# Full fp32 products between the fp32r products of a first job: one row of eight against four pairs

## The chip, the cores and the metric

One core of one Trainium2 chip runs the kernel. The metric is device time in microseconds. The kernel before took 410.91 us, the median of three runs from 410.29 to 411.19.

## The reference

The input `x` has 1024 tokens of 512 features. Two layers follow each other, each a residual sum and a layer norm:

```python
approx_up = x @ up_w.T ; gate_pre = x @ gate_w.T          # 128 columns each, the "first job"
delta = gate_pre - local_point
approx_out = approx_up @ local_approx_output.T
for m in 1..6:                                            # terms: delta^m / m! times approx_up
    approx_out += (term_m * approx_up) @ fuse_weight[:, :, m-1].T
ffn = (silu(x @ ffn_gate_w.T) * (x @ ffn_up_w.T)) @ ffn_down_w.T      # 1248 rows
x = layernorm(x + approx_out + ffn)
dq_i = nf4_quant_dequant(w_i)                             # blocks of 64, codes of 16 levels
x = layernorm(x + (silu(x @ dq1.T) * (x @ dq2.T)) @ dq3.T)            # 1376 rows
```

All is fp32, and nearly every product is made of three fp32r products: high part by high part, high by low and low by high.

## The kernel before

Each engine has a program of its own, written out by hand, and semaphores tie them together.

**TensorE (PE)** does, in this order: five warm-up products (L1426); the first job, which is `up` and `gate` of the term part over four chunks `c` of 128 features (chunk 0 by L1435, L1438 and L1441, chunks 1 to 3 by `product`, L1292 to L1294); then twenty pairs, `pair(1, i)`, each a half of 512 tokens of the gate and the up product of one group of rows of layer 1's feed-forward; then the passes of the second products; then the same for layer 2. A product here is a weight load of 128 columns and a matmul over 512 tokens.

The first group of rows is special. It has 96 rows of gate and 96 of up. Gate's 96 and the last 32 of up are one fp32r job (`project_first`, job `("in", 0)`); the other 64 rows of up aren't split at all but multiplied in full fp32, by `project_up` (L1325 to L1332). It makes eight matmuls, two for each chunk: tokens 0 to 511 go to the lower 64 partitions of bank 5 and tokens 512 to 1023 to the upper 64, so the two use different halves of PE's columns. The trace shows each such matmul as two records. They stand after `project_first` of pair 0, and only after the last of them is `s_pair` raised for pair 0 (L1359 to L1363). The weights, 256 columns of `raw`, come with job `("in", 0)` in one transfer of 768 columns.

**ScalarE (ACT)** makes high parts (`w_hi`, `x_hi`, `l_hi`, all at L597 by `copy`), the silu of each pair (L680) and the lines of the NF4 steps (`side`, L635 and L597). **GpSimd (POOL)** makes low parts of weights (`w_lo`, L1236) and of `h` (L1247), multiplies layer 2's gate by up (L1254), and for NF4 the normalising (L1208) and the clamps (`level`, L1217). **VectorE (DVE)** multiplies layer 1's gate by up (L917 for the first two pairs, L920 after), makes the terms and adds up NF4 levels (L881, L885). **SyncE (SP)** issues nearly all transfers in one queue.

**What sets the order of the NF4 work.** The 136 NF4 steps (17 units of 8) have no place of their own. At each place where an engine would do a piece of the main work it first calls `beside()`, which does so many steps as the next number of a table, `SHARE`, says. There is one list for ACT, one for DVE and one for POOL.

PE may start pair `i` of layer 1, from the fourth pair on, when the product `h` of pair `i - 3` is made (L1346 to L1348), since it takes the banks of that pair. With `i = 3` it waits for two products of `h`.

## Time and profile before

| | us |
|---|---|
| median of three runs | 410.91 |
| lowest, highest | 410.29, 411.19 |
| the profiled execution | 410.27 |
| its span, first to last instruction | 408.2 |
| around the span | 2.1 |
| PE busy | 399.9 |
| POOL busy | 289.8 |
| DVE busy | 324.3 |
| ACT busy | 267.0 |

A row of the timeline gives the start, the length, the engine, the line, what was written and read, and in square brackets how long the engine sat idle before it and what released it. A matmul of 512 tokens is shown with 0.39 us although the next one starts 0.23 us later: they overlap in the pipe. So times on PE are read from starts to starts or from ends to ends. PEld is PE's weight load.

### The profile page before, as it was taken

Reading aid. Unit: us, or ns where it says so; the run is one execution under the profiler, and the core shown is the slowest. Engines: PE = TensorE matmul, PEld = TensorE weight load, DVE = VectorE, ACT = ScalarE, POOL = GpSimd, SP = SyncE. Lnnn points to the kernel's source line nnn. Section 1 sums busy time; section 2 is a strip of 40 time slices with the busy share of each in tenths; the row PEclk is TensorE's granted clock in tenths of the full one; section 3 lists DMA queues with packets and bytes.
Section 4 is the critical chain, followed back from the end, with each engine's and each line's share of the span. In section 5 each row is a group of like instructions: output and inputs, shape, how many; then the busy total and the mean of one; then the engine's idle time right before and its main releaser. Section 6 shows DMA issues by size and latency. Waiting matters only on the chain.

```text
span 408.2 us, 5342 instructions
## 1 busy us (share of the span) xinstructions
PE 399.9 (98%) x1762; PEld 325.8 (80%) x1762; DVE 324.3 (79%) x385; ACT 267.0 (65%) x372; POOL 289.8 (71%) x228
## 2 busy tenths in 40 slices
PE   8999999999999999999999999999999999999993
PEld 6767888888888888888888888888888877888872
DVE  4539889789889996999969799887789989925035
ACT  5574676686685847466955668887769777732613
POOL 0177998986978499737992465799999998954330
PEclk9999999999999999999999999999999999999998
DMA  8993111000104362003052000000000000000202
GB/s 276 406 408 126 53 22 51 28 26 0 53 20 116 92 213 71 26 0 104 1 167 112 0 2 0 0 2 0 2 2 0 2 0 0 2 1 0 104 0 103
DMA packets 10010, 26.42 MB, mean 65 GB/s; under 512 B 1248, under 2 KB 1632, under 8 KB 9728
## 3 DMA queue, kind: packets, MB, share of 16 engines
q1 hardware_dynamic: 9552, 25.30, 17.9%
q10 hardware_dynamic: 432, 0.79, 0.7%
q8 instruction: 14, 0.23, 0.2%
q14 instruction: 12, 0.10, 0.1%
HBM read 23.99 MB, written 2.10 MB: 64 GB/s over the span
## 4 chain that ended last, share of the span: by engine, by line
PE 95%; DVE 1%; POOL 1%; ACT 1%; issue 0%; POOLq 0%; DVEq 0%; ACTq 0%
PE PS L1292 31%; PE PS L1294 31%; PE PS L1293 31%; PE PS L1426 1%; PE PS L1330 1%; PE PS L1420 1%; POOL level L1217 1%; DVE h L917 0%; POOLq L262 0%; PE PS L1435 0%; DVE PS L885 0%; ACT side L635 0%; ACT side L597 0%; PE PS L1438 0%; PE PS L1441 0%
## 5 line engine op out<-in xcount | busy, mean ns | idle before, releaser
L1217 POOL TENSOR_SCALAR level<-side 128x1024 f32<-128x1024 int8 (+2 forms) x119 | 129.0, 1084 | 27.7 <-ACT side L597 15.4
L885 DVE TENSOR_TENSOR PS<-PS,level 128x1024 f32<-128x1024 f32 (+2 forms) x102 | 120.1, 1178 | 22.6 <-POOL level L1217 18.8
L1292 PE MATMUL PS<-x_hi,w_hi 128*128 128x512 f32 (+1 forms) x340 | 132.7, 390 | 0.3 <-DVE h L917 0.3
L1294 PE MATMUL PS<-x_hi,w_lo 128*128 128x512 f32 (+1 forms) x340 | 132.4, 389 | 0.0
L1293 PE MATMUL PS<-x_lo,w_hi 128*128 128x512 f32 (+1 forms) x340 | 132.3, 389 | 0.0
L597 ACT ACTIVATE side<-Q 128x1024 int8<-128x1024 f32 (+2 forms) x84 | 80.6, 998 | 22.1 <-DVE PS L881 18.0
L1247 POOL TENSOR_TENSOR l_lo<-h,l_hi 128x512 fp32r<-128x512 f32 (+1 forms) x42 | 57.3, 1374 | 26.5 <-ACT l_hi L597 25.8
L1292 PEld LDWEIGHTS PS<-x_hi,w_hi 128*128 128x128 f32 (+1 forms) x340 | 63.4, 186 | 15.1 <-issue 0.8
L1294 PEld LDWEIGHTS PS<-x_hi,w_lo 128*128 128x128 f32 (+1 forms) x340 | 63.4, 186 | 13.8
L1293 PEld LDWEIGHTS PS<-x_lo,w_hi 128*128 128x128 f32 (+1 forms) x340 | 63.4, 186 | 13.6
L1293 PE MATMUL PS<-x_lo,l_hi 128*128 128x512 f32 (+1 forms) x144 | 56.1, 389 | 0.0
L1292 PE MATMUL PS<-x_hi,l_hi 128*128 128x512 f32 (+1 forms) x144 | 56.1, 389 | 0.0
L1294 PE MATMUL PS<-x_hi,l_lo 128*128 128x512 f32 (+1 forms) x144 | 56.0, 389 | 0.0
L1236 POOL TENSOR_TENSOR w_lo<-raw,w_hi 128x1024 fp32r<-128x1024 f32 (+2 forms) x15 | 30.8, 2051 | 19.6 <-ACT w_hi L597 19.0
L680 ACT ACTIVATE h<-PS 128x512 f32<-128x512 f32 (+1 forms) x42 | 24.9, 592 | 29.1 <-PE PS L1294 25.9
L1254 POOL TENSOR_TENSOR h<-h,Q 128x512 f32<-128x512 f32 (+1 forms) x22 | 30.3, 1378 | 18.0 <-ACT Q L597 15.7
L597 ACT ACTIVATE l_hi<-h 128x512 fp32r<-128x512 f32 (+1 forms) x42 | 25.9, 626 | 24.9 <-PE PS L1294 24.8
L597 ACT ACTIVATE side<-raw 128x1024 int8<-128x1024 f32 x35 | 35.1, 1058 | 6.1 <-DVE PS L881 6.1
L1292 PEld LDWEIGHTS PS<-x_hi,l_hi 128*128 128x128 f32 (+1 forms) x144 | 27.0, 188 | 6.0 <-issue 0.2
L1292 PE MATMUL PS<-w_hi,l_hi 128*128 128x512 f32 (+1 forms) x80 | 31.5, 394 | 0.2 <-POOL l_lo L1247 0.2
L1294 PEld LDWEIGHTS PS<-x_hi,l_lo 128*128 128x128 f32 (+1 forms) x144 | 27.0, 188 | 5.7
L1293 PEld LDWEIGHTS PS<-x_lo,l_hi 128*128 128x128 f32 (+1 forms) x144 | 27.0, 188 | 5.5
(103 smaller groups left out, 515.2 us busy)
## 6 DMA issues: line engine op xcount, KB each, us to landing
Q<-w SPq DMA_DIRECT2D x10, 512.0 KB, 13.9
raw<-w_in SPq DMA_DIRECT2D x9, 512.0 KB, 9.9
raw<-w_out SPq DMA_DIRECT2D x13, 256.0 KB, 2.7
raw<-w SPq DMA_DIRECT2D x5, 512.0 KB, 3.9
R<-xN SPq DMA_DIRECT2D x2, 1024.0 KB, 6.4
raw<-w_fuse SPq DMA_DIRECT2D x7, 256.0 KB, 2.5
out<-R SPq DMA_DIRECT2D x7, 256.0 KB, 2.0
h<-xT SPq DMA_DIRECT2D x2, 512.0 KB, 7.0
```

The source lines that it names most:

```text
L597: return nc.scalar.activation(dst, src, ACT.Copy, **kw)
L680: nc.scalar.activation(dst, PS[0:dst.shape[0], bank, :], ACT.Silu).then_inc(s_silu, 1)
L885: v.tensor_tensor(total, total, level_of(s), ALU.add).then_inc(s_add, 1)
L1217: g.tensor_scalar(level_of(s), side_of(s), LIMITS[k][1], LIMITS[k][0], ALU.min, ALU.max).then_inc(s_level, 1)
L1236: g.tensor_tensor(lo, w_raw(j)[0:p, 0:n], hi.bitcast(F32), ALU.subtract).then_inc(s_wlo_in if JOBS[j][0] == "in" else s_wlo, 1)
L1247: g.tensor_tensor(lo, view, hi.bitcast(F32), ALU.subtract).then_inc(s_llo_h, 1)
L1254: g.tensor_tensor(dst, dst, up2[0:dst.shape[0], k % 2, :], ALU.mult).then_inc(s_h2, 1)
L1292: t_.matmul(dst, a_hi, b_hi, start=start, stop=False)
L1293: t_.matmul(dst, a_hi, b_lo, start=False, stop=False)
L1294: return t_.matmul(dst, a_lo, b_hi, start=False, stop=stop)
L1330: last = t_.matmul(PS[half * LEFT:(half + 1) * LEFT, UP_BANK, :], w[:, c, :], xT_raw[:, c, half * HALF:(half + 1) * HALF], start=c == 0, s ...
L1420: last = t_.transpose(PS[:, XT_BANK + t % 2, c * P:(c + 1) * P], R[:, t, c * P:(c + 1) * P], ident[:])
```

## The change

`project_up` is cut in four. Each call now makes the two matmuls of one chunk: chunk 0 after chunk 0 of the first job, chunk 1 after its chunk 1, chunk 2 after its chunk 2, and chunk 3 after the whole first job, before pair 0. `s_pair` is raised for pair 0 right after `project_first`. The 256 columns of weights have a transfer of their own, `up_raw`, which stands in SP's queue ahead of the second half of the first job's weights; the transfer of job `("in", 0)` has 512 columns left. A new semaphore, `s_up_made`, tells SP when the weights may be overwritten, in place of pair 0. All three lists of `SHARE` have new numbers with the same sum of 136.

```diff
 SHARE = {
     "scalar": [
-        0, 0, 0, 4, 0, 4, 1, 0, 3, 0, 2, 0, 0, 3, 0, 1, 2, 2, 1, 1, 3, 1, 0, 4, 4, 0, 1, 3, 0, 3, 3, 0, 3, 0,
+        0, 0, 0, 1, 2, 1, 2, 0, 1, 0, 5, 0, 0, 1, 0, 4, 0, 1, 3, 0, 3, 4, 0, 2, 4, 0, 2, 4, 0, 2, 2, 0, 4, 0,
...
                     if j - RAW_SLOTS == JOB["in", 0]:
 
-                        wait_pairs_done(sp, 1, 1)
+                        sp.wait_ge(s_up_made, 1)
                 p, n = job_shape(j)
                 if kind == "in":
                     first = 2 * DC * first_row1(f)
+                    if f == 0:
+
+                        n = DC * P
                     src = w_in[:, first:first + n]
...
                 if c == 2:
+                    sp.dma_start(up_raw, w_in[:, DC * P:2 * DC * REST]).then_inc(s_up_raw, 16)
                     sp.dma_start(w_raw(0)[:, 2 * PRE0:1024], w_pre[:, 2 * PRE0:1024]).then_inc(s_raw[0], 16)
...
-            def project_up():
-
-                w = w_raw(JOB["in", 0])[:, DC * P:2 * DC * REST].rearrange("p (c m) -> p c m", c=DC)
-                for c in range(DC):
-                    for half in range(2):
-                        last = t_.matmul(PS[half * LEFT:(half + 1) * LEFT, UP_BANK, :], w[:, c, :],
-                                         xT_raw[:, c, half * HALF:(half + 1) * HALF], start=c == 0, stop=c == DC - 1)
+            def project_up(c):
+
+                w = up_raw.rearrange("p (c m) -> p c m", c=DC)
+                for half in range(2):
+                    pe.wait_ge((s_x, s_xb)[half if c < 2 else 0][c], 16)
+                    last = t_.matmul(PS[half * LEFT:(half + 1) * LEFT, UP_BANK, :], w[:, c, :],
+                                     xT_raw[:, c, half * HALF:(half + 1) * HALF], start=c == 0, stop=c == DC - 1)
                 return last
...
                 if layer == 1 and i < 2:
-                    last = project_first(half, bank)
-                    if half == 0:
-                        last = project_up()
-                    last.then_inc(s_pair, 1)
+                    project_first(half, bank).then_inc(s_pair, 1)
                     return
...
             for c in range(1, DC):
+
+                if c == 1:
+                    pe.wait_ge(s_up_raw, 16)
+                project_up(c - 1)
                 if c == 1:
                     pe.wait_ge(s_pre_hi, 2)
                     pe.wait_ge(s_pre_lo, 2)
...
+            project_up(DC - 1).then_inc(s_up_made, 1)
             for i in range(2 * C1):
                 pair(1, i)
```

On PE before, the eight fp32 matmuls (`PS<-h,raw`, since the unsplit x lies in `h`) follow the last products of pair 0:

```order
L1292 MATMUL PS<-x_hi,w_hi 128x512
L1293 MATMUL PS<-x_lo,w_hi 128x512
L1294 MATMUL PS<-x_hi,w_lo 128x512
L1330 MATMUL PS<-h,raw 64x512 x8
L1292 MATMUL PS<-x_hi,w_hi 128x512
L1293 MATMUL PS<-x_lo,w_hi 128x512
```

On PE now, the first of the four pairs stands between chunk 0 (L1440 to L1446) and chunk 1 (L1300 to L1302) of the first job:

```order
L1440 MATMUL PS<-x_hi,w_hi 128x512 x2
L1443 MATMUL PS<-x_hi,w_lo 128x512 x2
L1446 MATMUL PS<-x_lo,w_hi 128x512 x2
L1338 MATMUL PS<-h,raw 64x512 x2
L1300 MATMUL PS<-x_hi,w_hi 128x512
L1301 MATMUL PS<-x_lo,w_hi 128x512
```

One row of eight has become four rows of two, with products of 128 columns before and behind each. The other three stand 12, 24 and 36 products further on.

On ACT before, around the first two silus (`h<-PS 96x512`), four NF4 lines stand between them:

```order
L597 ACTIVATE w_hi<-raw 128x1024
L680 ACT_TABLE_LOAD
L680 ACTIVATE h<-PS 96x512
L635 ACTIVATE side<-Q,line 128x1024
L597 ACTIVATE side<-Q 128x1024 x3
L680 ACTIVATE h<-PS 96x512
L597 ACTIVATE w_hi<-raw 128x1024
```

On ACT now, at the same place:

```order
L605 ACTIVATE w_hi<-raw 128x1024
L688 ACT_TABLE_LOAD
L688 ACTIVATE h<-PS 96x512
L643 ACTIVATE side<-Q,line 128x1024
L688 ACTIVATE h<-PS 96x512
L605 ACTIVATE side<-Q 128x1024 x2
L605 ACTIVATE w_hi<-raw 128x1024
```

Three of the four lines have left the place ahead of the second silu.

On DVE before, at the multiplications of gate by up of the first two pairs (L917, two instructions for each pair), two additions of NF4 levels stand ahead of pair 1's:

```order
L917 TENSOR_TENSOR h<-PS,h 32x512
L917 TENSOR_TENSOR h<-PS,h 64x512
L881 SCALAR_TENSOR_TENSOR PS<-side,level 128x1024
L885 TENSOR_TENSOR PS<-PS,level 128x1024
L917 TENSOR_TENSOR h<-PS,h 32x512
L917 TENSOR_TENSOR h<-PS,h 64x512
```

On DVE now, at the same place (L917 has become L925):

```order
L925 TENSOR_TENSOR h<-PS,h 32x512
L925 TENSOR_TENSOR h<-PS,h 64x512
L925 TENSOR_TENSOR h<-PS,h 32x512
L925 TENSOR_TENSOR h<-PS,h 64x512
L1101 SCALAR_TENSOR_TENSOR R<-R 128x2x512
```

Both additions have moved behind pair 1's multiplications.

## Rows read from the trace of the kernel before

**Rows 1.** The page: busy time by engine; the granted clock by slice.

```profile
PE 399.9 (98%) x1762; PEld 325.8 (80%) x1762; DVE 324.3 (79%) x385; ACT 267.0 (65%) x372; POOL 289.8 (71%) x228
...
PEclk9999999999999999999999999999999999999998
```

**Rows 2.** The waits of PE: line, waited for, us in total, times, longest.

```profile
PE PS L1426 <- POOL level L1257: 1.2, 1, 1.2
PE PS L1292 <- DVE h L917: 0.3, 1, 0.3
PE PS L1292 <- POOL l_lo L1247: 0.2, 1, 0.2
```

**Rows 3.** Timeline around the fp32 matmuls: start us, length us, engine, line.

```profile
19.18 0.39 PE L1293 MATMUL PS<-x_lo,w_hi 128*128 128x512 f32 x1
...
19.41 0.39 PE L1294 MATMUL PS<-x_hi,w_lo 128*128 128x512 f32 x1
19.73 0.20 PEld L1330 LDWEIGHTS PS<-h,raw 128*64 128x64 f32 x4 [0.35 <-issue]
19.73 3.65 PE L1330 MATMUL PS<-h,raw 128*64 128x512 f32 x16
20.21 0.14 PEld L1330 LDWEIGHTS PS<-h,raw 128*64 128x64 f32 x2 [0.29 <-issue]
...
22.36 0.14 PEld L1330 LDWEIGHTS PS<-h,raw 128*64 128x64 f32 x2 [0.28 <-issue]
...
23.31 0.50 PE L1292 MATMUL PS<-x_hi,w_hi 128*128 128x512 f32 x1
```

**Rows 4.** Timeline of PE around eight transposes of 128 columns.

```profile
192.59 0.39 PE L1294 MATMUL PS<-x_hi,l_lo 128*128 128x512 f32 x1
192.82 1.04 PE L1420 MATMUL PS<-ident,R 128*128 128x128 f32 x8
193.61 0.48 PE L1292 MATMUL PS<-w_hi,l_hi 128*128 128x512 f32 x1
```

**Rows 5.** Timeline of PE where the fourth pair of layer 1 begins.

```profile
31.38 0.39 PE L1294 MATMUL PS<-x_hi,w_lo 128*128 128x512 f32 x1
32.05 0.50 PE L1292 MATMUL PS<-x_hi,w_hi 128*128 128x512 f32 x1 [0.29 <-DVE h L917]
```

**Rows 6.** Timeline of ACT around the first two silus.

```profile
23.43 0.59 ACT L680 ACTIVATE h<-PS 96x512 f32<-96x512 f32 x1 [3.04 <-PE PS L1330]
23.92 1.14 ACT L635 ACTIVATE side<-Q,line 128x1024 int8<-128x1024 f32 x1
...
27.81 0.58 ACT L680 ACTIVATE h<-PS 96x512 f32<-96x512 f32 x1
```

**Rows 7.** Timeline of DVE: the multiplications of pair 1.

```profile
30.59 1.40 DVE L917 TENSOR_TENSOR h<-PS,h 32x512 f32<-32x512 f32 x2
```

**Rows 8.** Timeline of POOL: its first low part and first normalising.

```profile
19.17 2.37 POOL L1236 TENSOR_TENSOR w_lo<-raw,w_hi 128x1024 fp32r<-128x1024 f32 x1 [18.02 <-ACT w_hi L597]
21.49 1.90 POOL L1208 TENSOR_TENSOR Q<-Q,rcp 128x1024 f32<-128x1024 f32 x1
```

**Rows 9.** Timeline of ACT and PE while x and the first weights arrive.

```profile
7.74 0.63 ACT L597 ACTIVATE x_hi<-h 128x512 fp32r<-128x512 f32 x1 [0.37 <-DMA h<-xT]
...
8.76 0.39 PE L1292 MATMUL PS<-x_hi,w_hi 128*128 128x512 f32 x1
...
9.69 2.45 ACT L597 ACTIVATE x_hi<-h 128x512 fp32r<-128x512 f32 x4 [0.66 <-DMA h<-xT]
```

**Rows 10.** Timeline of PE at the last job of the last pass.

```profile
391.84 0.39 PE L1294 MATMUL PS<-x_hi,l_lo 128*128 128x512 f32 x1
...
392.43 0.47 PE L1292 MATMUL PS<-w_hi,l_hi 96*128 96x512 f32 x1 [0.20 <-POOL l_lo L1247]
```

**Rows 11.** Timeline of POOL: the low part of weights that the ninth pair takes.

```profile
56.74 2.39 POOL L1236 TENSOR_TENSOR w_lo<-raw,w_hi 128x1024 fp32r<-128x1024 f32 x1
```

**Rows 12.** Timeline of PE where the ninth pair begins.

```profile
59.39 0.39 PE L1292 MATMUL PS<-x_hi,w_hi 128*128 128x512 f32 x1
```

More of the change, by code:

```diff
@@ L326, in l_slot @@
             return l_hi[0:p, n % L_SLOTS, :], l_lo[0:p, n % L_SLOTS, :]
+        up_raw = w_raw(JOB["in", 0])[:, DC * P:2 * DC * REST]
         def job_shape(j):
@@ L363, in build @@
         s_lhi, s_llo_t, s_llo_h = sem("s_lhi"), sem("s_llo_t"), sem("s_llo_h")
+        s_up_raw, s_up_made = sem("s_up_raw"), sem("s_up_made")
         s_pre, s_up, s_delta = sem("s_pre"), sem("s_up"), sem("s_delta")
```

22 rows, old and new, of the table SHARE are left out of this document.

## The prediction, made before the changed kernel ran

> **What bounds the kernel now.** I read the page's first part first: PE is busy 399.9 us of a span of 408.2, the next engine, DVE, 324.3 [rows 1]. The waits of PE come second. Only three have a releaser: 1.2 us at the start, 0.3 for DVE in layer 1's pairs, 0.2 for POOL at the end [rows 2]. So the kernel is a string of PE work with almost no holes. A change can win only by taking work or a hole off PE, and loses what it adds there. The granted clock is at the top in nearly every slice [rows 1], and PE's work in the first microseconds stays as it is up to the first moved matmul, so I expect nothing from the clock.
>
> How large are the two holes inside? I take them from end to end, since ends follow each other by 0.23 us in the steady stream. At the fourth pair: (32.05 + 0.50) - (31.38 + 0.39) - 0.23 = **0.55 us** [rows 5]. At the last job: (392.43 + 0.47) - (391.84 + 0.39) - 0.23 = **0.44 us** [rows 10].
>
> **What the fp32 matmuls cost.** They take no time from anything else on PE, so their price is what they insert. From the last product before to the first behind, (23.31 + 0.50) - (19.41 + 0.39) - 0.23 = 3.78 us [rows 3]. Inside they are eight steps: the weight loads come by twos, at 20.21 and five steps on at 22.36, so a step is 0.43 us, and eight are 3.44 [rows 3]. Sixteen records in eight steps means that two always run together. What is left, 3.78 - 3.44 = **0.34 us**, is the price of going in and out once. Its signs are in the rows: the first loads start at 19.73, after 0.35 us without a load, and the product behind is shown with 0.50 us in place of 0.39 [rows 3].
>
> **Four visits in place of one.** The number of fp32 matmuls is the same, two for each chunk, thus two steps of 0.43. Each pair of them now stands between products of 128 columns, so the 0.34 is paid four times: a pair costs 0.86 + 0.34 = 1.20, four cost 4.80, against 3.78. That is **+1.02 us**, all on PE and so on the path.
>
> Is 0.34 the price of one visit however short? The lower bound is zero. Eight transposes between ordinary products insert (193.61 + 0.48) - (192.59 + 0.39) - 0.23 = 0.88 us, 0.11 each, which leaves next to nothing for going in and out [rows 4]; but they use all 128 columns, and the fp32 matmuls use 64. The upper bound is that two matmuls alone don't overlap as in a row of eight: four steps of 0.43 and 0.34 are 2.06 for a pair, 8.24 for four, which is +4.46. I take 0.34, since those rows are of the same instructions, and the first two records of the row already run together (four loads within the 0.20 us from 19.73 [rows 3]), without a predecessor of their own kind.
>
> The traced rows show a hole of 0.34 us around the 64-column matmuls and hardly one around the 128-column transposes. The Trainium skill, "TensorEngine Tiling (Array Packing)", section "Key Properties", says that changing the tiling mode, not just the tile, drains TensorE. It speaks against this change and gives no figure; if each change of mode drains, the sum is the +1.02 above, and if only long rows paid for it, 0.
>
> **The waits that the change adds on PE.** The first pair now waits for its weights. They are 128 KB in the same queue, ahead of the second half of the first job's weights. From 7.74, when the second half of x's chunk 1 is in, to 9.69, when chunk 2 is in, 256 KB of weights and 512 KB of x landed [rows 9]; that is 394 KB/us, so 128 KB take 0.33 us and are there at about 8.1. PE gets to them when chunk 0 of the job is done, at 8.76 [rows 9]. The cover is 0.7 us; without it PE would wait for what is missing. What stands behind in the queue (the weights of chunks 2 and 3, then x's chunks 2 and 3) lands 0.33 later, and PE asks for it 1.20 later, so it has gained cover. The total of bytes is the same, so the queue has caught up after job ("in", 0). The waits for x itself are old news: its high parts were made from it.
>
> **Who is later now.** The first job ends 3 x 1.20 = 3.6 us later. ACT's copy of up, its `w_hi` and POOL's `w_lo` for the second group hang on that: `w_lo` was there at 19.17 + 2.37 = 21.5 [rows 8] and will be at 25.1. PE wants it for pair 2, 12 products of 0.23 us behind the one at 23.31 [rows 3], at 26.1, now at 27.1. The cover shrinks from 4.6 to 2.0 us, and nothing is lost. SP's wait for `s_up_made` ends earlier than that for pair 0, but its queue is still busy with NF4 weights, so it gives nothing.
>
> **The hole of 0.55 at the fourth pair.** PE waits there for `h` of pair 1, which was made at 30.59 + 1.40 = 32.0 [rows 7]. On ACT four NF4 lines stand before pair 1's silu, which ended at 27.81 + 0.58 [rows 6], and on DVE two additions stand before its multiplications. The new table has one line and no addition there. Walked by rows: the products of pair 0 ended at 19.80 and now end 4.80 later, at 24.6, its silu 0.59 after that [rows 3, 6], at 25.2; POOL's `w_lo` ends at 25.1, its normalising of 1.90 [rows 8] at 27.0; ACT's one line of 1.14 [rows 6] to 28.2; the silu of pair 1, for which PE is done at 24.6 + 12 x 0.23 = 27.4, to 28.8; DVE's 1.40 to 30.2. PE gets there at 31.38 + 0.23 + 1.02 = 32.6 [rows 5]. So 2.4 us of cover where 0.55 were missing: **-0.55 us**.
>
> **The rest of the tables.** Before, some covers are thin: `w_lo` of the ninth pair was ready at 56.74 + 2.39 = 59.13, and PE took it at 59.39 [rows 11, 12], 0.26 us. Now two POOL steps fewer stand before it, and PE comes 0.5 us later. In the first pass of layer 1, DVE has two additions fewer before the low parts of the terms. In layer 2 the counts run within four steps of the old ones. I find no place where a step was put before something thin, but can't walk all 136, so I leave +0.0 in the sum and widen the range. The hole of 0.44 at the end stays: no NF4 step is near it, and ACT and POOL can start there only when PE frees a slot.
>
> **The sum.** +1.02 - 0.55 = **+0.47 us**. The profiled execution took 410.27, so it would take 410.7; it lies 0.64 below the median of 410.91, within their spread. On the median: **411.4 us**.
>
> **Rivals.**
> 1. *The new tables bring a wait of their own.* Another hole like the 0.55, or two, opens in the 290 us of pairs and passes, where DVE and POOL are busy 79% and 71% of the span [rows 1] and covers of 0.26 us exist. For it: the old tables left one such hole. Against: at the thin places I looked at, the counts went down. Price: +0.47 and 0.5 to 1.5 more, 411.9 to 412.9, slower. It decides from 0.35 us of new waits on.
> 2. *Two alone don't overlap fully.* In a row of eight, each half of PE's columns always has its next matmul at hand. The second matmul of a pair now carries a wait, and its second record may run alone. One step more for each pair is 4 x 0.43 = 1.72, thus 413.1; two steps more, +3.44, give 414.8. Against: the first two records of the row overlap too [rows 3].
> 3. *Going in and out is cheap for a short visit.* Then only the -0.55 stays: 410.4, still within 0.2%. For it only the transposes speak [rows 4].
> 4. *Faster.* Case 3 and the hole at the end goes too: -0.99, 409.9. It needs both.
> 5. *The change doesn't do what it says*: PE waits for `up_raw` and loses the overlap with the arriving data. With a cover of 0.7 us out of 0.33 us of transfer I give it no chance of its own; it would add some tenths.
>
> **How the numbers follow.** Forecast 50%, of which a fifth ends above 411.7 by small new waits; rival 1 20%; rival 2 10%; rival 3 10%; rival 4 and what I don't see on that side 10%. What a measurement of this kernel can tell from no change is about 0.2%, 0.82 us. Slower by more: 10 + 20 + 10 = 40%. Faster by more: 10%. Within: 50%. The range leaves out most of rival 2's far end and of rival 4: 410.3 to 413.1.
>
> **What would show it.** Right: in the timeline, four groups of four fp32 records, each inserting 1.2 us between the products around it, and the first at 8.8 to 8.9; the first job's end 3.6 us later; no wait of PE for DVE at the fourth pair; PE's busy time up by about 1 us, its idle time down by half a microsecond. Wrong: an insertion near 0.9 (rival 3) or 1.6 and more (rival 2); a row for PE in the waits that wasn't there, by POOL `w_lo`, DVE `l_lo` or DVE `w_lo` (rival 1); a wait of PE for the transfer of `raw` near 9 us (rival 5).

## The result, and the profile after

The changed kernel took **419.58 us**, median of five runs from 418.78 to 420.29. The kernel before took 410.86 beside it, five runs from 410.25 to 411.19. The ratio is 1.0215, with a 95% interval of 1.0195 to 1.0235. The forecast was 411.4, with a range up to 413.1: the kernel is 8.7 us slower where half a microsecond was foreseen. The profiled execution spans 417.1 us, against 408.2.

The page of the kernel after, to be held against [rows 1]: busy time by engine, and the granted clock by slice of 10.4 us.

```profile
PE 402.9 (97%) x1762; PEld 326.4 (78%) x1762; DVE 328.7 (79%) x385; ACT 267.0 (64%) x372; POOL 294.4 (71%) x228
...
PEclk9999999999999999999987999999999999999998
```

PE is busy 3.0 us longer, with as many instructions, and idle about 6 us longer. At slices 21 and 22 the clock isn't at its top, as it was before. The waits of PE, against [rows 2]: line, waited for, us in total, times, longest.

```profile
PE PS L1300 <- POOL l_lo L1255: 5.4, 3, 4.8
PE PS L1431 <- POOL level L1265: 1.2, 1, 1.2
PE PS L1440 <- ACT x_hi L605: 0.5, 1, 0.5
PE PS L1300 <- issue: 0.4, 1, 0.4
```

The wait for DVE's `h` is gone. POOL's `l_lo` is now waited for three times, once for 4.8 us; of the short two, one is the hole at the end that was there before. The 0.5 us for ACT's `x_hi` stand ahead of the first product and cost nothing: the last row of chunk 0 starts at 8.29, before at 8.30. The timeline of PE at the first and the fourth visit of the fp32 matmuls, against [rows 3]: start, length, engine, line.

```profile
8.83 1.08 PE L1338 MATMUL PS<-h,raw 128*64 128x512 f32 x4
9.84 0.50 PE L1300 MATMUL PS<-x_hi,w_hi 128*128 128x512 f32 x1
...
20.39 0.39 PE L1302 MATMUL PS<-x_hi,w_lo 128*128 128x512 f32 x1
20.71 1.08 PE L1338 MATMUL PS<-h,raw 128*64 128x512 f32 x4
21.72 0.50 PE L1300 MATMUL PS<-x_hi,w_hi 128*128 128x512 f32 x1
```

Each visit is four records in two steps. The last inserts (21.72 + 0.50) - (20.39 + 0.39) - 0.23 = 1.21 us, where 1.20 was foreseen. The three that start at 12.79, 16.75 and 20.71 are alike to the hundredth, and the first comes to 1.21 too. Four make 4.84 in place of 3.78: 1.06 us, where 1.02 was foreseen.

The timeline of PE where the time went:

```profile
214.03 0.39 PE L1302 MATMUL PS<-x_hi,l_lo 128*128 128x512 f32 x1
219.18 0.77 PE L1300 MATMUL PS<-x_hi,l_hi 128*128 128x512 f32 x1 [4.76 <-POOL l_lo L1255]
219.74 0.63 PE L1301 MATMUL PS<-x_lo,l_hi 128*128 128x512 f32 x1
...
222.73 0.63 PE L1302 MATMUL PS<-x_hi,l_lo 128*128 128x512 f32 x1
223.15 0.47 PE L1300 MATMUL PS<-x_hi,l_hi 128*128 128x512 f32 x1
```

The hole is (219.18 + 0.77) - (214.03 + 0.39) - 0.23 = **5.3 us** from end to end. Behind it eight products follow each other by 0.427 us in place of 0.228, and the ninth by 0.27: the clock stands at 1.2 GHz, half of its upper level, until 223.2. That is **1.6 us** more. The stretches of 1.7, 3.5 and 3.5 us there: busy time of PE, PEld, DVE, ACT and POOL with the number of instructions, then the granted clock, the DMA share and GB/s.

```profile
218.00:219.70 1.70, 0.52 (x1) 0.50 (x2) 1.59 (x2) 0.00 (x0) 1.62 (x2) 0.50 0.19 61
219.70:223.20 3.50, 3.50 (x10) 2.68 (x9) 3.50 (x5) 3.38 (x4) 3.34 (x3) 0.50 0.02 5
223.20:226.70 3.50, 3.50 (x17) 2.89 (x16) 2.84 (x7) 1.63 (x3) 2.15 (x3) 0.98 0.01 2
```

PE is fully busy in the second and third, but does 10 products in one and 17 in the other, at clocks of 0.50 and 0.98.

Two smaller holes are new:

```profile
81.47 0.39 PE L1302 MATMUL PS<-x_hi,w_lo 128*128 128x512 f32 x1
82.26 0.47 PE L1300 MATMUL PS<-x_hi,w_hi 128*128 128x512 f32 x1 [0.40 <-issue]
...
163.77 0.39 PE L1302 MATMUL PS<-w_hi,l_lo 128*128 128x512 f32 x1
164.65 0.47 PE L1300 MATMUL PS<-w_hi,l_hi 128*128 128x512 f32 x1 [0.49 <-POOL l_lo L1255]
```

They are 0.64 and 0.73 us. The sum: 1.06 for the visits, -0.55 for the hole at the fourth pair, 0.64 + 0.73, 5.3 and 1.6 make **8.8 us**, of 8.9 between the two spans.

**Back from the hole.** ACT's part of the chain:

```profile
216.15 1.02 ACT L605 ACTIVATE w_hi<-PS 128x1024 fp32r<-128x1024 f32 x1 [7.33 <-DVE PS L1036]
217.07 0.62 ACT L605 ACTIVATE l_hi<-h 128x512 fp32r<-128x512 f32 x1
```

PE waits for `l_lo`, that for `l_hi`. On ACT `l_hi` stands in the queue behind `w_hi`, which waited 7.33 us for a transpose on DVE. Its last microseconds on DVE:

```profile
202.23 2.07 DVE L852 TENSOR_REDUCE amax<-Q 128x16 f32<-128x1024 f32 x2
204.34 7.71 DVE L859 TENSOR_SCALAR rcp<-amax 128x32 f32<-128x32 f32 x1
212.08 0.35 DVE L861 RECIPROCAL rcp<-rcp 128x32 f32<-128x32 f32 x1
...
214.85 1.26 DVE L1036 STREAM_TRANSPOSE PS<-Q 128x1024 f32<-128x1024 f32 x1
```

Here is the cause's root: a `TENSOR_SCALAR` on 32 values per partition takes **7.71 us**. It is the floor of the block maxima (they are raised to the least normal number before the reciprocal). The same instruction in the kernel before:

```profile
201.55 0.64 DVE L851 TENSOR_SCALAR rcp<-amax 128x32 f32<-128x32 f32 x1
```

With POOL idle it takes 0.18 us, as at 73.73 in the kernel after. POOL in the kernel after at that time, and then in the kernel before:

```profile
199.98 1.90 POOL L1225 TENSOR_SCALAR level<-side 128x1024 f32<-128x1024 int8 x1
201.96 1.30 POOL L1255 TENSOR_TENSOR l_lo<-h,l_hi 96x512 fp32r<-96x512 f32 x1
203.22 1.30 POOL L1244 TENSOR_TENSOR w_lo<-raw,w_hi 128x512 fp32r<-128x512 f32 x1
204.48 1.29 POOL L1255 TENSOR_TENSOR l_lo<-h,l_hi 128x512 fp32r<-128x512 f32 x1
...
210.73 1.28 POOL L1244 TENSOR_TENSOR x_lo<-raw,x_hi 128x512 fp32r<-128x512 f32 x1
217.76 1.27 POOL L1255 TENSOR_TENSOR l_lo<-h,l_hi 128x512 fp32r<-128x512 f32 x1 [5.75 <-ACT l_hi L605]
```

```profile
202.09 1.29 POOL L1247 TENSOR_TENSOR l_lo<-h,l_hi 128x512 fp32r<-128x512 f32 x1
203.33 1.30 POOL L1236 TENSOR_TENSOR x_lo<-raw,x_hi 128x512 fp32r<-128x512 f32 x1
204.72 1.04 POOL L1217 TENSOR_SCALAR level<-side 128x1024 f32<-128x1024 int8 x1
```

In the kernel after the floor ends at 212.05, and POOL's six low parts from 204.48 on, which follow each other without a gap, end at 210.73 + 1.28 = 212.01. The new table has moved one clamp (`level<-side`) four places forward in POOL's row: it stood at 204.72, now it is the one at 199.98. The floor is a single-source instruction from SBUF to SBUF, and all of POOL's are in SBUF. The Trainium skill, "SBUF — State Buffer", section "Who interferes with whom", says that such an instruction of DVE in its two-port mode and GpSimd's share a port pair, that whoever issues first gets it for the whole instruction, and that the other fully blocks. That gives one instruction of waiting. The trace agrees with it at the other places (0.64 us above, and 1.28 at 152.38 in the kernel after, each to the end of the POOL instruction under way), but six more in a row are more than it says.

### The profile page after: what moved, and what is told of

It reads as the page before. It is cut to its first block, busy times and chain, and to the rows that moved or that the text cites. A ratio compares the mean times of both kernels' runs of the same rounds, so it can differ in the third digit from the quotient of the medians.

```text
span 417.1 us, 5344 instructions
## 1 busy us (share of the span) xinstructions
PE 402.9 (97%) x1762; PEld 326.4 (78%) x1762; DVE 328.7 (79%) x385; ACT 267.0 (64%) x372; POOL 294.4 (71%) x228
## 4 chain that ended last, share of the span: by engine, by line
PE 90%; issue 4%; POOL 3%; DMA 1%; DVE 1%; ACT 0%; POOLq 0%; DVEq 0%; ACTq 0%
PE PS L1300 30%; PE PS L1302 29%; PE PS L1301 29%; POOL l_lo L1255 2%; PE PS L1338 1%; DMA raw<-w_pre 1%; POOL x_lo L1244 1%; PE PS L1425 1%; POOL level L1225 1%; POOL w_lo L1244 0%; POOLq L262 0%; PE PS L1440 0%; PE PS L1443 0%; PE PS L1446 0%; ACT R L605 0%
## 5 line engine op out<-in xcount | busy, mean ns | idle before, releaser
L1225 POOL TENSOR_SCALAR level<-side 128x1024 f32<-128x1024 int8 (+2 forms) x119 | 131.5, 1105 | 36.8 <-DVE PS L893 14.7
L1300 PE MATMUL PS<-x_hi,w_hi 128*128 128x512 f32 (+1 forms) x340 | 133.1, 391 | 0.4 <-issue 0.4
L1302 PE MATMUL PS<-x_hi,w_lo 128*128 128x512 f32 (+1 forms) x340 | 132.4, 389 | 0.0
L1300 PEld LDWEIGHTS PS<-x_hi,w_hi 128*128 128x128 f32 (+1 forms) x340 | 63.4, 186 | 17.5 <-issue 3.2
L1302 PEld LDWEIGHTS PS<-x_hi,w_lo 128*128 128x128 f32 (+1 forms) x340 | 63.4, 186 | 13.9
L1300 PE MATMUL PS<-x_hi,l_hi 128*128 128x512 f32 (+1 forms) x144 | 57.0, 396 | 4.8 <-POOL l_lo L1255 4.8
L1302 PE MATMUL PS<-x_hi,l_lo 128*128 128x512 f32 (+1 forms) x144 | 56.8, 394 | 0.0
L1244 POOL TENSOR_TENSOR w_lo<-raw,w_hi 128x1024 fp32r<-128x1024 f32 (+2 forms) x15 | 31.8, 2117 | 22.4 <-ACT w_hi L605 21.7
L1300 PEld LDWEIGHTS PS<-x_hi,l_hi 128*128 128x128 f32 (+1 forms) x144 | 27.6, 191 | 11.0 <-issue 5.2
L1300 PE MATMUL PS<-w_hi,l_hi 128*128 128x512 f32 (+1 forms) x80 | 31.6, 396 | 0.7 <-POOL l_lo L1255 0.7
L1302 PEld LDWEIGHTS PS<-x_hi,l_lo 128*128 128x128 f32 (+1 forms) x144 | 27.5, 191 | 5.8
```

Source lines behind the costliest of these rows:

```text
L1225: g.tensor_scalar(level_of(s), side_of(s), LIMITS[k][1], LIMITS[k][0], ALU.min, ALU.max).then_inc(s_level, 1)
L1244: g.tensor_tensor(lo, w_raw(j)[0:p, 0:n], hi.bitcast(F32), ALU.subtract).then_inc(s_wlo_in if JOBS[j][0] == "in" else s_wlo, 1)
L1300: t_.matmul(dst, a_hi, b_hi, start=start, stop=False)
L1302: return t_.matmul(dst, a_lo, b_hi, start=False, stop=stop)
```

## The experiments

`SHARE` is the table that deals the NF4 steps out; an index is a place at which an engine takes so many steps. The ratios below are to runs of the kernel before on the same chip, whose medians lay between 410.44 and 410.72.

### Splitting the change in two

**The new order of PE with the old tables.**

```diff
-SHARE = { ... }    # the tables of after
+SHARE = { ... }    # the tables of before
```

> The changed kernel with the old tables: the four pairs of fp32 matmuls and the transfer of their own, but every NF4 step where it was. Theory S (a short VectorE instruction, the floor of the scales, waits while GpSimd runs a long row of two-input instructions, and the new tables made that row): the floor takes under 1.2 us again, no hole near 219 us, the four pairs insert 4.80 us in place of 3.78, and the wait at the fourth pair is back: 410.9 + 1.0 = 411.9 us. Rival O (the order of the fp32 matmuls itself brings the loss): 417 us or more.

Measured: 415.36, ratio 1.011 (1.0095 to 1.0125). The long floor isn't there (at most 1.13 us), but the time is 3.5 us above what was expected. PE and then ACT of this kernel:

```profile
35.21 0.50 PE L1300 MATMUL PS<-x_hi,w_hi 128*128 128x512 f32 x1 [2.40 <-DVE h L925]
...
36.52 0.63 PE L1302 MATMUL PS<-x_hi,w_lo 128*128 128x512 f32 x1
```

```profile
27.07 1.15 ACT L643 ACTIVATE side<-Q,line 128x1024 int8<-128x1024 f32 x1 [1.78 <-POOL Q L1216]
```

The hole at the fourth pair, 0.55 in [rows 5], is now 2.66 us. POOL's `w_lo` for the second group hangs on the end of the first job and comes 3.6 us later, and its normalising behind it; so ACT's first line begins at 27.07 and not at 23.92 [rows 6], 3.15 later, and with it the silu of pair 1 and DVE's multiplications. PE itself comes only 1.02 later: 0.55 + 3.15 - 1.02 = 2.68. The old table's four lines ahead of that silu can't stay with the new order; the forecast walked this chain for the new table alone. Some 1.3 us behind the hole the clock falls, and eight products from 36.52 on are at half speed, which adds 1.6. With 1.06 and 2.1 that is 4.8 us, as between the spans of 413.0 and 408.2.

**The new tables with the old order.**

```diff
-SHARE = { ... }    # the tables of before
+SHARE = { ... }    # the tables of after
```

> The kernel before with the new tables: the eight fp32 matmuls in one row behind pair 0. Theory S, if it hangs on the tables alone: the floor again takes 6 to 8 us, TensorE waits near 218 us, 418 to 419 us. Rival O: 410.4 us, the wait at the fourth pair gone and nothing else. Between the two, if the row of GpSimd is there but the floor comes at another moment of it: 410.4 plus what is left of the wait.

Measured: 418.58, ratio 1.0191 (1.0176 to 1.0206). The floor takes 7.72 us, the hole at 218.2 is 5.2 us, ten products behind it are slow. So the tables alone bring nearly all of the loss. The kernel after is 1.00 us above this one, and its span 0.9. That is near the 1.06 of the four visits, but the intervals leave about 1 us of play, and this kernel's hole at 81.3 is 1.02 us where the kernel after has 0.64. So the price of the visits rests on the rows above and not on this difference.

### Is it the floor, and is it the clamp?

**No floor.** This kernel leaves out the floor of the maxima of `w1` and `w2`; the reciprocal reads the maxima.

```diff
-                v.tensor_scalar(inverse, maxima, TINY, None, ALU.max).then_inc(s_floor, 1)
-                dve.wait_ge(s_floor, scaled(group[-1]))
-                v.reciprocal(inverse, inverse).then_inc(s_prep, 1)
+                v.reciprocal(inverse, maxima).then_inc(s_prep, 1)
```

> The changed kernel, its reciprocals for w1 and w2 read the maxima themselves; the floor of the scales (128x32, a guard against a block of zeros) is left out. Theory S: no hole near 219 us, no slow matmuls behind it; the 5.3 us and about 1.8 us of the lower clock go, 419.6 - 7.1 = 412.5 us. Rival L (the late low part of h is due to GpSimd's or ScalarE's own load, the long floor only stands beside it): at least 417 us.

Measured: 412.57, ratio 1.0046 (1.0029 to 1.0063). The hole at 219 and the slow products are gone, 7.0 us in all. The six floors left out take 0.18 us each where nothing holds them up. Holes of 0.36 and 0.34 us at 81.8 and 163.8 stay, and one of 0.9 at 181 is new.

**The clamp back in its old place.**

```diff
-SHARE["gpsimd"][34], SHARE["gpsimd"][38] = 1, 0
+SHARE["gpsimd"][34], SHARE["gpsimd"][38] = 0, 1
```

> The changed kernel with one number of GpSimd's table moved back: the clamp that stood between the low parts of the rows of out 0 and 1 in the kernel before stands there again, so the row of seven two-input instructions is cut in two. Theory S: the floor ends when the clamp comes, after about 4 us in place of 7.7, and TensorE's hole of 5.3 shrinks to under 2: 413 to 415 us. Rival R (what instruction GpSimd runs doesn't matter, only that it runs without a gap): the floor still takes 7 us or more, about 419.6 us.

Measured: 412.93, ratio 1.0055 (1.0038 to 1.0071). One step moved, in tables of 415 numbers, gives 6.7 of the 8.7 us back. The floor of this kernel:

```profile
204.00 0.63 DVE L859 TENSOR_SCALAR rcp<-amax 128x32 f32<-128x32 f32 x1
```

It got in as soon as the `l_lo` under way had ended, with the next low part ready behind it. The clamp, at 205.93, came later than that; it can't have been what opened the door.

**The floor three places later.** DVE's step that holds it goes behind the low parts of x and the transpose.

```diff
-SHARE["vector"][70], SHARE["vector"][73] = 3, 0
+SHARE["vector"][70], SHARE["vector"][73] = 2, 1
```

> The changed kernel, with one number of DVE's row moved: the NF4 step that holds the small floor of the scales (the 128x32 TENSOR_SCALAR that took 7.71 us at 204.34) comes three places later, behind the low parts of x and the transpose that wait in line after it; POOL's row is not touched, so its train of six low parts in a row stays. My theory (DVE is shut out of its small one-source instruction for as long as POOL's two-input low parts follow each other without a gap, and all behind it on DVE, then ACT, then POOL's l_lo, then PE, is late): the floor no longer meets the train, or meets it where nothing urgent stands behind; the hole of 5.3 us at 219 goes, and with it the half-clock products (1.75). 419.6 - 7.0 = 412.6, within 412.3 to 413.5. Rival A (the train itself is what makes PE wait, as POOL is behind by its own work, and the long floor is a symptom): the hole stays, 418 to 420. Rival B (the floor is long wherever it stands near POOL's work): a hole of several us at another place, 415 and more.

Measured: 415.36, ratio 1.0118 (1.0104 to 1.0132). Rival B's case: the floor met POOL's row at 209.14, took 4.09 us, to the end of what was left of the row, and the wait moved to DVE's `x_lo` and to the layer norm.

### What keeps the floor out?

Now the theory was that a row of POOL's without a gap shuts it out. It was put to the test by itself, with segments put behind the last store of the kernel before.

```diff
+            # POOL, ten times: a row of eight to twenty instructions
+            g.tensor_tensor(h[:, i * 512:i * 512 + 512], level[:, 0, 0:512], level[:, 1, 0:512], ALU.subtract)
+            # DVE, when the second has ended:
+            v.tensor_scalar(rcp[:, 0:1, :], amax[:, 0:1, :], TINY, None, ALU.max)
```

> The kernel before, and behind its last store ten short segments with nothing else running, which change no output. In each POOL runs a row of instructions without a gap (T: TENSOR_TENSOR 128x512 from two operands in SBUF, 1.25 us each; C: the clamp, a TENSOR_SCALAR 128x1024 from int8, 1.1 us each), and when POOL's second one is done, DVE gets one instruction to issue. Segments: 1 ten T, DVE the floor (TENSOR_SCALAR 128x32 SBUF to SBUF); 2 four T, a C, five T, the floor; 3 ten T, RECIPROCAL 128x32; 4 ten T, TENSOR_TENSOR 128x32; 5 ten T, the floor's TENSOR_SCALAR with its source in PSUM; 6 eight C, the floor; 7 ten T, TENSOR_SCALAR 128x512; 8 ten T, TENSOR_TENSOR 128x512 from two operands in SBUF; 9 ten T, two floors in a row; 10 twenty T, the floor. My theory (DVE's instruction is shut out until POOL's row has a gap or an instruction of another kind): in 1 the floor ends with the tenth T, about 10 us; in 2 with the C, 2.5 to 3.5 us; in 3 and 5 0.2 to 0.4 us; in 6 under 1.3 us; in 7 as 1; in 10 about 22 us. For 4 and 8 the trace shows low parts on DVE stretched from 0.69 to 1.6 us, so I expect up to a few us. In 9 the second floor is quick, since the row is over by then. Rival (POOL and DVE take turns, one instruction each, and the 7.71 us came from something else that was under way, such as a transfer or ACT): the floor takes at most 1.4 us in every segment.

The theory fell. DVE's instructions of segments 1, 3, 5 and 8: start, length.

```profile
411.09 1.15 DVE L1215 TENSOR_SCALAR rcp<-amax 128x16 f32<-128x16 f32 x1 [2.67 <-POOL h L1325]
...
435.97 0.25 DVE L1217 RECIPROCAL rcp<-amax 128x16 f32<-128x16 f32 x1 [11.32 <-POOL h L1325]
...
460.79 0.17 DVE L1221 TENSOR_SCALAR rcp<-PS 128x16 f32<-128x16 f32 x1 [11.30 <-POOL h L1325]
...
494.87 1.63 DVE L1225 TENSOR_TENSOR Q<-Q 128x512 f32<-128x512 f32 x1 [11.22 <-POOL h L1325]
```

The floor waits for the one instruction under way, and gets in ahead of POOL's next. So does a `TENSOR_TENSOR` of two SBUF operands. A `RECIPROCAL` and a floor that reads PSUM didn't wait. The section of the Trainium skill named above has two kinds of instruction contend, `tensor_scalar` in its two-port mode and `tensor_tensor` with both inputs in SBUF. The probe agrees with it on both, and on the length: one instruction. The section doesn't name `RECIPROCAL`.

**Does the moment of arrival decide?** Three runs asked that: a probe that swept it, and two kernels in which a dummy `RECIPROCAL` delays the floor.

```diff
+                v.reciprocal(Q[:, 5 + k // 5, at:at + n], Q[:, 4, at:at + n])    # n from 10 to 160
                 ins = v.tensor_scalar(rcp[:, 0:2, :], amax[:, 0:2, :], TINY, None, ALU.max)
```

> The kernel before, and behind its last store 27 short segments with nothing else running, which change no output. In each POOL runs eight TENSOR_TENSORs 128x512 in a row (SBUF, 1.22 us from start to start); when the second is done, DVE runs a RECIPROCAL over n elements as a delay and then the floor (TENSOR_SCALAR 128x32, SBUF to SBUF), so that the floor comes at a chosen age of POOL's instruction: n from 10 to 160, ages 0.3 to 1.2 us. Segments 17 and 18 take a TENSOR_TENSOR in place of the floor, 19 reads from PSUM, 20 to 27 repeat n = 100 to 142 with POOL writing fp32r behind a wait, as in the kernel. The last probe took from my theory that a row of POOL's instructions shuts the floor out as such: arriving 0.15 us after POOL's start it ended with that one instruction. What the traces of the kernels show is an age: arriving 0.04 to 0.06, 0.70 to 0.74 or 1.3 of 2.4 us after POOL's start the floor ended with that instruction; at 1.00 (e5, 4.09 us) and 1.12 (after and the tables alone, 7.71) it ended with the whole row; at 1.175 it slipped in and took 0.18. New theory (the age decides: one that comes when POOL's instruction is nearly done, with the next already asking, loses every turn): floors at ages 1.0 to 1.13 take 5 to 6 us, to the end of the eight, the others 1.22 minus the age. Rival (the age is not it; something of the kernel's own, such as waits, fp32r or work of ACT and DMA beside it, is needed): all floors take at most 1.3 us, or only those of 20 to 27 are long.

All 24 floors from SBUF got in after at most one instruction, at ages from 0.02 to 1.21 us (the age is the time since POOL's instruction under way had started). The row below has shortest, median and longest in ns, then the start of the first and the last.

```profile
L1211 DVE TENSOR_SCALAR rcp<-amax x24: 117/320/1020, 411.3 to 672.3; 128x32 f32<-128x32 f32 x24
```

```diff
                 if group == SCALE_GROUPS[-1]:
+                    v.reciprocal(delay[:, 1, 0:22], delay[:, 0, 0:22])
```

> The changed kernel with 0.2 us of idle work added: a RECIPROCAL over 22 elements, of which nothing is used, ahead of the two reductions that precede the long floor; tables and order stay. In the kernel after, the floor came 1.12 us after the start of POOL's TENSOR_TENSOR of 1.29 us, 0.14 before the next one's start, and took 7.71 us; floors that came at ages of 0.04 to 0.06 and 0.70 to 0.74 ended with that one instruction. Theory (the age decides in the kernel, though the probe did not show it): 0.2 later it comes 0.06 us after the start of the next one and takes 1.3 us; the hole at 219 goes, 412.3 to 413.5. Rival (this place, with its six low parts in a row, shuts it out at any age): 418.5 to 420.

Measured: 420.08, ratio 1.0238 (1.022 to 1.0255). The floor came some 0.15 us later against its neighbours: not 1.12 us into POOL's instruction but 0.01 into the next. It took 7.56 us.

The same, with 54 elements, in the kernel before:

> The kernel before with 0.4 us of idle work added, a RECIPROCAL over 54 elements ahead of the same two reductions. Its floor came at 201.55, 0.72 us after the start of POOL's TENSOR_TENSOR, and took 0.64 us. Theory (the age decides): now at an age of about 1.12, it loses every turn until POOL's clamp, which starts at 204.72 in this order: it takes 2.5 to 3.0 us. PE has cover for this there: 410.4 to 411.5. Rival (the age does not matter): 0.2 us or one instruction of POOL, at most 1.4 us, 410.4 to 410.8. The time hardly tells them apart, the length of the floor in the trace does.

Measured: 410.4, ratio 1.0006 (0.9992 to 1.0019). The floor came at an age of 1.08 us, near the 1.12 of the kernel after, and took 0.31. So age isn't it.

**Is it what the probe left out?** The third probe put a reduction and a semaphore ahead of the floor, gave POOL's instructions fp32r outputs and waits of their own, and let ACT copy beside them.

```diff
+                v.tensor_reduce(amax[:, 0, 0:12], Q[:, 3, 0:768].rearrange("p (b e) -> p b e", e=BLOCK), AX_X, ALU.max,
+                                apply_absolute_value=True).then_inc(s_red, 1)
+                dve.wait_ge(s_red, k + 1)
                 ins = v.tensor_scalar(rcp[:, 0:2, :], amax[:, 0:2, :], TINY, None, ALU.max)
```

> The kernel before, and behind its last store 26 segments that change no output, made more like the place in the kernel: the floor has a TENSOR_REDUCE 128x768 ahead of it and waits for it by a semaphore. POOL runs eight TENSOR_TENSORs 128x512; the first one's end starts DVE, which runs a RECIPROCAL over n elements (10 to 176), the reduction and the floor, so that ages from 0.1 to 1.2 us are met. 1 to 10: POOL as in the last probe. 11 to 18: POOL writes fp32r from two tensors, each instruction behind a wait of its own. 19 to 26: the same, with eight copies of 128x512 on ACT beside it. Theory (an age of 1.0 to 1.13, in conditions like the kernel's, loses every turn): at the ages near 1.1 the floor takes 4 to 6 us in all three kinds, or in the later ones alone, which then names the condition. Rival (a condition that this probe also lacks, such as PE or DMA): none over 1.3 us.

None of 26 took over 1.29 us. The rival holds.

**Is it the shared port?**

```diff
-v.tensor_scalar(inverse, maxima, TINY, None, ALU.max)
+v.tensor_scalar(*(t.rearrange("p u b -> p b u") for t in (inverse, maxima)), TINY, None, ALU.max)
```

> The changed kernel, complete, with the floor of the scales reading and writing its 128x32 values in another order: inner step 16 elements in place of 1. Nothing else moves. Theory (the floor waits because, contiguous and from SBUF to SBUF, it runs in a mode that needs the port that DVE shares with POOL): with a step it doesn't need the port, takes some 0.2 us at 204.3 although POOL's six low parts still stand beside it, and the hole of 5.3 us and the half-clock products go: 419.6 - 7.1 = 412.5, within 412.2 to 413.2. Rival (it is not the port but something else at this place that keeps the instruction for 7.7 us): the floor stays at 7 us and the time at 419 to 420.

Measured: 419.57, ratio 1.0216 (1.0199 to 1.0233); the floor took 7.72 us. That doesn't speak against the port, since the next probe showed that a step doesn't free the instruction from it: alone beside POOL's row, the stepped floor took 0.6 and 1.0 us like the other.

**Is it what came before?** In after, e2, e5, e8 and e10 the clamp ahead of the row had itself been held up by DVE (1.90 us for 1.04, at 199.98); where the floor got in, a low part had been.

```diff
+                # POOL: two low parts, then the clamp that DVE holds up, then eight low parts
+                v.scalar_tensor_tensor(sum_, side[:, 1, :], LIMITS[0][1], level[:, 2, :], ALU.min, ALU.add)
```

> The kernel before, and behind its last store 20 segments that change no output. In all four kernels in which the floor was shut out (after, the tables alone, e5, e8) POOL had, in the same run of work, a clamp (single source) that itself had been held up by a DVE instruction with two operands in SBUF (1.90 us in place of 1.04, at 200.0); where the floor passed (before, e1, e4, e9) a two-operand instruction of POOL had been held up (2.27 us). Each segment repeats that: POOL runs two TENSOR_TENSORs, then X, then eight more; DVE issues an instruction with two SBUF operands during the second (the addition that the kernel has, or a TENSOR_TENSOR), so that X is held up; then a RECIPROCAL, the reduction, a delay and the floor. 1 to 6: X is the clamp, 7 to 12: X is a TENSOR_TENSOR; in each three with the one holder and three with the other, delays 20, 90, 150. 13: a holder with one operand. 14 to 18: X the clamp, and in place of the floor a RECIPROCAL, a TENSOR_TENSOR, the floor from PSUM, the floor with a step (twice). 19, 20: the floor with other delays. Theory (a clamp held up leaves DVE out of turn from then on): floors of 1 to 6 and 19, 20 take 4 to 8 us, those of 7 to 12 at most 1.3. Rival (history does not matter either): none over 1.3 us. In both cases 14, 16, 17 and 18 take 0.1 to 0.4 us.

The clamps were held up as in the kernel, 1.90 us; no floor took over 1.18.

**One clamp in the kernels.** First the old kernel with the clamp where the new table has it, then the new kernel with the clamp one place further back:

```diff
-SHARE["gpsimd"][34], SHARE["gpsimd"][38] = 0, 1
+SHARE["gpsimd"][34], SHARE["gpsimd"][38] = 1, 0
```

> The kernel before with one number of POOL's row changed: the clamp that stands four places behind, between two l_lo, comes ahead of them, as in the new table; DVE's and ACT's rows and the fp32 matmuls stay. In this order POOL has six low parts in a row beside the floor. Theory (this one move is enough): the floor takes 5 to 8 us, PE waits some 4 to 5.5 us near 210 and runs some products at half clock, 410.6 + 5 to 7 = 415.5 to 418. Rival (it takes the other moved steps as well): floor at most 1.3 us, 410.4 to 411.5.

Measured: 411.36, ratio 1.0016 (1.0005 to 1.0027). The rival holds: the floor took 0.65 us, with a gapless row beside it that was longer than in the kernel after. The time is 0.6 us up, with a new hole of 0.8 us at 233.6, where PE waits for an `x_lo` of DVE's.

```diff
-SHARE["gpsimd"][34], SHARE["gpsimd"][35] = 1, 0
+SHARE["gpsimd"][34], SHARE["gpsimd"][35] = 0, 1
```

> The changed kernel with the same clamp one place further back (behind the next l_lo, ahead of w_lo), so that it is no longer the instruction that DVE's addition holds up; behind it there are still six low parts in a row beside the floor. Theory A (that the clamp was held up at 200.0 is the condition for the long floor): the floor takes at most 1.3 us, 412.5 to 413.5. Theory B (the row of six without a clamp is the condition, in the kernel if not in the probes): the floor takes 6 to 8 us and the time is 418.5 to 420.

Measured: 412.26, ratio 1.0048 (1.0032 to 1.0065), 7.3 us less for one clamp moved by one place. DVE and POOL of this kernel:

```profile
203.87 0.33 DVE L859 TENSOR_SCALAR rcp<-amax 128x32 f32<-128x32 f32 x1
```

```profile
201.74 1.05 POOL L1225 TENSOR_SCALAR level<-side 128x1024 f32<-128x1024 int8 x1
202.87 1.30 POOL L1244 TENSOR_TENSOR w_lo<-raw,w_hi 128x512 fp32r<-128x512 f32 x1
204.12 1.30 POOL L1255 TENSOR_TENSOR l_lo<-h,l_hi 128x512 fp32r<-128x512 f32 x1
...
211.63 1.29 POOL L1255 TENSOR_TENSOR l_lo<-h,l_hi 128x512 fp32r<-128x512 f32 x1
```

The floor slipped in between `w_lo` and `l_lo`, with seven low parts still to come in a row, no clamp among them. A gapless row beside the floor is therefore not enough, in the kernel either. That fits theory A of this run, for which the next two runs brought no proof.

```diff
-SHARE["gpsimd"][32], SHARE["gpsimd"][38] = 0, 1
+SHARE["gpsimd"][32], SHARE["gpsimd"][38] = 1, 0
```

> The kernel before with the same clamp moved two places further forward than in e11, ahead of the l_lo that DVE's addition of two SBUF operands holds up there (2.28 us at 196.9 in e11), so that it is the clamp that is held up; behind it come three l_lo, then w_lo and the row beside the floor. Theory A (a clamp held up, and nothing of DVE's that needs the shared port between it and the floor, is the condition; so it was in all five kernels with the long floor and in none of the others): the floor takes 4 to 8 us, PE waits, 413 to 419. Rival (the condition is another): the floor takes at most 1.3 us, 410.7 to 412.

Measured: 412.69, ratio 1.0054 (1.0038 to 1.0071), floor 0.53 us. The run tells nothing about its question: POOL came to the clamp when DVE had just finished, and it wasn't held up (1.04 us). The time is 2.2 us above the kernel before, with new holes of 0.95 and 0.8 us at 201 and 234.

```diff
+                # DVE beside that row, in the kernel's own order:
+                v.tensor_tensor(sum_, sum_, level[:, 0, :], ALU.add).then_inc(s_held, 1)
+                v.tensor_reduce(amax[:, 1, :], ...)
+                v.tensor_reduce(amax[:, 0, 0:12], ...)
```

> The kernel before, and behind its last store 18 segments that repeat the place at 198 to 212 us of the kernel after as closely as can be done with PE and the transfers idle, and change no output. POOL: two TENSOR_TENSORs, X, one of 96 partitions, eight more, all from the tensors of the kernel, fp32r out, each behind a wait. DVE: the addition of two SBUF operands that holds X up, the addition of the level into PSUM (which waits for X), the two reductions, a delay of 0 to 150 elements, the floor. 1 to 7: X the clamp, ACT idle; 8 to 14: the same with ACT copying beside it; 15, 16: X a TENSOR_TENSOR; 17, 18: a RECIPROCAL in place of the level's addition. Theory A: floors of 4 to 8 us in 1 to 14 and none in 15 and 16. Rival (the condition lies with PE, the transfers or something else that the probes lack): none over 1.3 us; then the cause stays open.

Clamp held up 1.89 us, then the row, then the floor:

```profile
L1237 DVE TENSOR_SCALAR rcp<-amax x18: 117/540/1137, 416.4 to 685.6; 128x32 f32<-128x32 f32 x18
```

**What stays open.** In four probes 83 floors of 128x32 met a row of POOL's, and the longest took 1.29 us. In five kernels, in every timed run by their times, one floor at the same place took 4.1 to 7.7. Ruled out as the condition by themselves are a gapless row, the moment of arrival, fp32r outputs and waits on POOL, copies on ACT, and a clamp held up before. Nor did the shorter hold-up of a clamp in the kernel after at 149.60 (1.40 us) bring it: the floor at 152.38 took 1.28. The probes had PE and the transfers idle, which wasn't tried otherwise. Nor was a floor that reads PSUM put in the kernel's place, which would show whether the shared port alone holds it there. Why POOL kept the turn six times is not known.

### Can the old hole be closed?

The forecast counted -0.55 for the hole at the fourth pair. In the kernel before it can be closed by itself, by one addition on DVE:

```diff
-SHARE["vector"][3], SHARE["vector"][4] = 2, 0
+SHARE["vector"][3], SHARE["vector"][4] = 1, 1
```

> The kernel before, with one number of DVE's row moved: of the two NF4 additions ahead of pair 1's multiplications one goes behind them; nothing else. In the trace of before PE waited 0.55 us at the fourth pair for these multiplications, which began 1.2 us late behind that addition. Theory: the hole goes and nothing else changes, 410.6 to 410.8 - 0.55 = 410.1. Rival (the addition given back later makes another thing late, as the new tables did): 410.6 and above, with a new hole in the trace of PE.

Measured: 410.63, ratio 1.0002 (0.9993 to 1.0011). The hole at 32 is gone, and this is new:

```profile
59.68 0.47 PE L1292 MATMUL PS<-x_hi,w_hi 128*128 128x512 f32 x1 [0.27 <-issue]
```

It is 0.50 us, at the ninth pair, whose `w_lo` had been ready 0.26 us ahead [rows 11, 12]. This profiled execution runs 0.45 us late from the start (chunk 1's first product at 9.21, before at 8.76). Taken from there, `w_lo` was ready at the same time as before (59.58 against 59.13), and PE came some 0.55 earlier than it. The gain stopped at the next thin cover. With this one mended too:

```diff
-SHARE["vector"][3], SHARE["vector"][4], SHARE["vector"][10], SHARE["vector"][13] = 2, 0, 1, 2
+SHARE["vector"][3], SHARE["vector"][4], SHARE["vector"][10], SHARE["vector"][13] = 1, 1, 0, 3
-SHARE["gpsimd"][4], SHARE["gpsimd"][6] = 3, 6
+SHARE["gpsimd"][4], SHARE["gpsimd"][6] = 2, 7
```

> The kernel before with two places mended: the NF4 addition ahead of pair 1's multiplications goes behind them (as in e6), and at the ninth pair the clamp ahead of POOL's l_lo and w_lo, with its addition on DVE, goes behind w_lo. In e6 the 0.55 us gained at the fourth pair came back as 0.50 us at the ninth, since w_lo there had been ready 0.26 us ahead of PE and PE now came earlier. Theory: w_lo ends 1.1 us earlier, both holes are gone, 410.5 - 0.55 = 409.95. Rival (each hole closed opens the next behind it, as something else has no cover either): 410.4 to 410.7 with a new hole further on.

Measured: 414.39, ratio 1.01 (1.0083 to 1.0117). Both holes are gone, and five others are there, of 0.3 to 1.5 us, the two largest at 76.8 and 105.6:

```profile
PE PS L1292 <- issue: 1.3, 1, 1.3
PE PS L1292 <- DVE h L920: 1.2, 1, 1.2
```

The only edit against e6 is one clamp and its addition a few places later; which of the steps behind them they made late was not followed further. No version was found that beats the kernel before.

## Why the prediction was wrong

- **The insertion.** Right, at 1.21 us a visit against 1.20, and 1.06 for all four against 1.02. Going in and out costs 0.34 us each time, for a visit of two steps as for one of eight. Rivals 2 and 3 fall. The Trainium skill, "TensorEngine Tiling (Array Packing)", section "Key Properties", says that a change of tiling mode drains TensorE; the trace agrees, with 0.34 us around each visit.
- **The transfer.** It cost nothing in the profiled execution after, but the cover of 0.7 us wasn't there. In that execution PE's weight loads stood still 0.35 us ahead of the first fp32 matmul, as long as before the other three visits. In the kernel without the floor PE came some 0.5 us earlier and did wait for `up_raw`. The weight loads of the one and the other (idle time in square brackets):

```profile
8.83 0.20 PEld L1338 LDWEIGHTS PS<-h,raw 128*64 128x64 f32 x4 [0.35 <-DMA raw<-w_in]
```

```profile
8.60 0.20 PEld L1336 LDWEIGHTS PS<-h,raw 128*64 128x64 f32 x4 [0.59 <-DMA raw<-w_in]
```

The first visit of that kernel inserted 1.45 us, and that of the kernel with the delay of 22 elements 1.48. So in these two the weights came at about 8.6 to 8.7, not at 8.1. Rival 5, which got no chance of its own, costs a quarter of a microsecond in some executions.

- **The hole at the fourth pair.** Right: -0.55. DVE's multiplications ended at 28.82 + 1.40 = 30.22, where 30.2 was worked out. The run with the old tables shows that the new row was needed there, or 2.66 us would have been lost.
- **The rest of the tables, "+0.0 in the sum".** This is the step that failed. It was argued from counts: within four steps of the old ones, nothing put before something thin. But the sum of a row is not its effect. One clamp, four places forward, was 6.7 of the 8.7 us in the company of the other moved steps; in the old tables the same move costs 0.6. And POOL's `w_lo` at 79.76, now behind a normalising and three clamps where one clamp stood, and the `l_lo` at 163.2 were another 1.4. At the first of them steps were put before something thin after all. The forecast looked at what stands before what PE waits for, and not at which instructions of DVE and POOL now meet.
- **The hole at the end.** Right: it stays, at 401.25, with 0.43 us.
- **The price of rival 1**, "0.5 to 1.5 more". Its kind was right, a wait of PE for POOL's `l_lo` that wasn't there before. Its size was taken from the holes that the old trace showed, while nothing bounded it: the trace of before has floors of 0.64 and 1.13 us beside a normal 0.18, which said that this instruction can be held up.
- **"I expect nothing from the clock".** Wrong by 1.6 us. That was argued for PE's first microseconds alone. The hole of 5.3 us here, and that of 2.7 with the old tables, took the clock down behind them.

## What to carry to other kernels

Where a table deals hundreds of steps anew, the change is the table: walk every place at which a row differs, or put the chance of a new long wait high and its price at several microseconds. Look also for small instructions in the trace that are now and then several times as long as usual, since what holds them up a little in one order can hold them up for long in another, and ask what queues behind them. And a hole closed in a chain with thin covers gives its time back only up to the next one.

## What the runs showed of the hardware

- A `TENSOR_SCALAR` of DVE on 32 values a partition, from SBUF to SBUF, takes 0.12 to 0.18 us when nothing holds it up. Beside POOL it ended with the instruction under way, 1.29 us at most in the probes, and in one place of five kernels it was kept out for three to six more, up to 7.7 us. A step in its operands didn't free it. Beside the same rows `RECIPROCAL` 128x32 took 0.29 us, `TENSOR_REDUCE` 128x768 0.89 to 0.94, with hardly a spread, and a floor of 16 values from PSUM 0.10 to 0.18: these didn't wait.
- Behind a hole of 5.3 us PE's granted clock was at 1.2 GHz for 4 us of work, behind one of 2.7 us it fell some 1.3 us after PE had started again and stayed down for 3.4; 1.6 us were lost each time. The two holes of 1.5 us, at 76.8 and 105.6 with both old holes closed, showed no slow products behind them.
- A pair of fp32 matmuls of 64 columns between products of 128 costs two steps of 0.43 and 0.34 us for going in and out, as much as a row of eight pays once.
